# The additive band mask of a windowed attention, entered into PSUM by eight 64x32 tiles instead of two full-array products

## What is computed

```python
def local_attention(q, k, v):           # WINDOW = 32
    ...
    mask = (it < jb) | (it > jb + w) | (jb == -1)
    sim = jnp.einsum('bhwie,bhwje->bhwij', bq, bk2) * QK_SCALE
    sim = jnp.where(mask, -jnp.finfo(sim.dtype).max, sim)
    attn = jax.nn.softmax(sim, -1)
    out = jnp.einsum('bhwij,bhwje->bhwie', attn, bv2)
for i in range(DEPTH):                  # 6
    x = attn_layer(shift_tokens(x), Wqkv[i], q_scale[i], k_scale[i], Wo[i]) + x
    x = ffn_layer(shift_tokens(x), ln_g[i], ln_b[i], W1[i], b1[i], W2[i], b2[i]) + x
```

## Time and profile before

| | |
|---|---|
| median of 3 runs (lowest, highest) | 1658.93 us (1653.15, 1659.83) |
| the profiled execution, its own time | 1655.81 us |
| its span, first to last instruction | 1654.0 us |
| mean granted TensorE clock | 0.979 of full |
| busy share: PE, ACT, POOL, DVE | 90%, 79%, 77%, 74% |
| PE matmuls (and as many weight loads) | 28624 |
| chain that ended last: PE, ACT, DVE, POOL, issue | 51%, 32%, 5%, 5%, 5% |

### The profile page before, as it was taken

The page is one execution under the profiler, slowest core; times in us unless marked ns, Lnnn a source line. Parts: engine busy times, 40 slices in busy tenths (PEclk is TensorE's granted clock), DMA queues, the critical chain, the costliest instruction groups (busy, mean ns, idle before and its releaser), DMA issues.

```text
span 1654.0 us, 68231 instructions
## 1 busy us (share of the span) xinstructions
PE 1485.1 (90%) x28624; PEld 1207.0 (73%) x28624; DVE 1223.0 (74%) x2376; ACT 1314.5 (79%) x4789; POOL 1279.5 (77%) x1540
## 2 busy tenths in 40 slices
PE   6588999999899899999888999999999899999985
PEld 4467777787677688777777777777777777777874
DVE  6676886887687877768876777878688677777762
ACT  3387887987888888878878888888788797887883
POOL 4388787887787888877978878778779787887761
PEclk9699999999999999999999999999999999999998
DMA  4011220112121121212111212112122012111111
GB/s 128 10 48 52 60 56 27 48 49 58 53 62 28 49 58 46 67 35 55 41 42 47 70 41 56 47 30 66 45 66 56 22 41 60 39 41 47 29 47 33
DMA packets 51021, 80.70 MB, mean 49 GB/s; under 512 B 8962, under 2 KB 16948, under 8 KB 50716
## 3 DMA queue, kind: packets, MB, share of 16 engines
q1 hardware_dynamic: 50716, 76.34, 16.6%
HBM read 18.69 MB, written 1.05 MB: 12 GB/s over the span
## 4 chain that ended last, share of the span: by engine, by line
PE 51%; ACT 32%; DVE 5%; POOL 5%; issue 5%; DMA 0%; SPq 0%; DVEq 0%; POOLq 0%
ACT pr L659 13%; PE ps L424 8%; ACT sq L625 5%; PE ps L401 5%; PE ps L408 5%; PE ps L452 4%; PE ps L462 4%; PE ps L434 4%; PE ps L493 4%; PE ps L402 4%; PE ps L403 4%; ACT pT L665 3%; ACT kT L650 3%; PE ps L418 3%; ACT qT L650 3%
## 5 line engine op out<-in xcount | busy, mean ns | idle before, releaser
L799 POOL TENSOR_TENSOR t<-t 128x512 f32<-128x512 f32 x384 | 498.8, 1299 | 203.9 <-DVE t L984 203.8
L659 ACT ACTIVATE pr<-ps,nmax 128x64 f32<-128x64 f32 x1536 | 475.4, 362 | 1.2 <-DVE nmax L999 1.2
L820 POOL TENSOR_TENSOR t<-t,rn 128x512 f32<-128x512 f32 x384 | 392.7, 1044 | 7.5
L659 ACT ACTIVATION_READ_ACCUMULATOR pr<-ps,nmax 128x1 f32 x1536 | 381.1, 257 | 0.0
L982 DVE TENSOR_TENSOR t<-ps,rope 128x512 f32<-128x512 f32 x384 | 263.0, 685 | 144.9 <-PE ps L408 75.0
L625 ACT ACTIVATE sq<-ps 128x512 f32<-128x512 f32 x384 | 240.4, 646 | 60.6 <-PE ps L403 60.0
L401 PE MATMUL ps<-w_hi,xt_hi 128*128 128x512 f32 x576 | 270.7, 470 | 17.0 <-DVE t L984 5.5
L961 DVE TENSOR_REDUCE sums<-sq 128x8 f32<-128x512 f32 x384 | 249.7, 666 | 19.9 <-ACT sq L625 19.9
L984 DVE TENSOR_TENSOR t<-ps,rope 128x512 f32<-128x512 f32 x384 | 261.3, 680 | 0.0
L402 PE MATMUL ps<-w_lo,xt_hi 128*128 128x512 f32 x576 | 230.5, 400 | 1.4 <-issue 1.4
L403 PE MATMUL ps<-w_hi,xt_lo 128*128 128x512 f32 x576 | 231.1, 401 | 0.3 <-issue 0.3
(11 more groups left out here) (123 smaller groups left out, 2764.4 us busy)
## 6 DMA issues: line engine op xcount, KB each, us to landing
v_win<-v SPq DMA_DIRECT2D x384, 128.0 KB, 2.3
wqkv<-wqkv_in SPq DMA_DIRECT2D x36, 256.0 KB, 3.9
xsh<-xr SPq DMA_DIRECT2D x24, 224.0 KB
wo<-wo_in SPq DMA_DIRECT2D x6, 512.0 KB, 3.4
w<-w_in SPq DMA_DIRECT2D x6, 342.0 KB, 4.4
w<-w_in SPq DMA_DIRECT2D x6, 172.5 KB
x<-x_in SPq DMA_DIRECT2D x4, 256.0 KB, 5.9
out<-x SPq DMA_DIRECT2D x4, 256.0 KB, 2.7
```

The costliest lines, as they stand in the source:

```text
L659: i = A(pr[:, c, odd * SPAN:(odd + 1) * SPAN], ps[:, S_BANK[odd], c * SPAN:(c + 1) * SPAN], ACT.Exp, bias=nmax[:, odd, c:c + 1], accum_out ...
L799: G.tensor_tensor(t1[:, c, :], t1[:, c, :], t2[:, c, :], ALU.add).then_inc(qk_added[c], 1)
L820: G.tensor_tensor(w, w, rn[:, par(u), h2, a, :].unsqueeze(2).broadcast_to([P, 8, E]), ALU.mult).then_inc(done, 1)
```

## The change

The mask is entered in the same eight parts of the array as the scores. The part with rows 0 to 63 must give queries 64 to 127 their mask too (groups 2 and 3), and the part with rows 64 to 127 must give it to queries 0 to 63. So the constants get a second copy of the mask with its halves swapped (`np.roll(band, P // 2, 0)`), and `band16` holds both. Per unit there are eight matmuls of 512 columns, each with 64 rows and 32 columns of the array, instead of two on the whole array. The constants' transfer grows from 96 to 128 KB, DVE makes two casts instead of one, and POOL's wait for all constants ahead of its steps goes.

```diff
-    return (0.5 * rope).astype(np.float32), np.concatenate([band, ident], 1)
+    return (0.5 * rope).astype(np.float32), np.concatenate([band, ident, np.roll(band, P // 2, 0)], 1)
-    consts = sb("consts", [P, SPAN + P])
+    consts = sb("consts", [P, SPAN + P + SPAN])
-    band16 = sb("band16", [P, BLOCKS, SPAN], BF16)
+    band16 = sb("band16", [P, 2, BLOCKS, SPAN], BF16)
...
-                for odd in range(2):
-                    mm(ps[:, S_BANK[odd], :], ident16[:], band16[:].rearrange("p c w -> p (c w)"), start=True, stop=False,
-                       skip_group_check=True)
+                for g in range(P // WIN):
+                    for odd in range(2):
+                        r, q = slice(E * odd, E * odd + E), slice(WIN * g, WIN * g + WIN)
+                        rows = slice(E * odd + WIN * (g % 2), E * odd + WIN * (g % 2) + WIN)
+                        mm(ps[q, S_BANK[odd], :], ident16[r, rows], band16[r, int(g // 2 != odd)].rearrange("p c w -> p (c w)"),
+                           start=True, stop=False, skip_group_check=True)
...
-            pool.wait_ge(const_ready, 9)
...
-            V.tensor_copy(band16[:], consts[:, 0:SPAN].unsqueeze(1).broadcast_to([P, BLOCKS, SPAN])).then_inc(const_ready, 1)
+            for k, c in enumerate((0, SPAN + P)):
+                V.tensor_copy(band16[:, k], consts[:, c:c + SPAN].unsqueeze(1).broadcast_to([P, BLOCKS, SPAN])).then_inc(const_ready, 1)
```

More of the change, by code:

```diff
@@ L285, in shift_tokens @@
                 else:
-                    sp.wait_ge(const_ready, 9)
+                    sp.wait_ge(const_ready, 10)
                 for t, n in SHIFT_PARTS:
@@ L574, in _ @@
             pe.wait_ge(ld_const, 64)
-            pe.wait_ge(const_ready, 9)
+            pe.wait_ge(const_ready, 10)
             cross_transpose(0)
@@ L721, in _ @@
             A(ident16[:], ident, ACT.Copy).then_inc(const_ready, 1)
-            act.wait_ge(const_ready, 9)
+            act.wait_ge(const_ready, 10)
             cross_copy_inputs(0)
@@ L1087, in _ @@
             dve.wait_ge(ld_const, 64)
-            V.tensor_copy(band16[:], consts[:, 0:SPAN].unsqueeze(1).broadcast_to([P, BLOCKS, SPAN])).then_inc(const_ready, 1)
+            for k, c in enumerate((0, SPAN + P)):
+                V.tensor_copy(band16[:, k], consts[:, c:c + SPAN].unsqueeze(1).broadcast_to([P, BLOCKS, SPAN])).then_inc(const_ready, 1)
             cross_normalise_x(0)
-            dve.wait_ge(const_ready, 9)
+            dve.wait_ge(const_ready, 10)
             cross_stats_x(1)
```

## The result

The kernel after took 1667.0 us (median of 8 runs, 1663.96 to 1679.2), the kernel before 1659.63 (8 runs, 1653.15 to 1666.58). The ratio is 1.0053, with a 95% interval of 1.003 to 1.0076: slower by half a per cent, 7 us, just over what counts here as no change. The forecast was 1655 with 1642 to 1668.

A forecast was written before the change was run, and what follows sets the result against it. ACT's loop was taken to pace light steps, PE those with feed-forward work. A 13.2 us gain in 56 clean units less 9.1 of losses gave 1651.7 for the profiled execution, 1655 against the median, range 1642 to 1668.

The forecast's parts named there:

- What the mask costs and will cost: First mask to first score on PE: 0.52 us falls to 0.24; gain 0.28 where PE waited, 0.19 elsewhere.
- the passage: PE's switch from the whole array to its parts, 0.09 us; the change moves it ahead of the mask, not away.
- rival 3: The masks issue slowly, 0.06 us each: gain near 0.03 us per clean unit, 1666 us; chance 0.04.
- rival 4: The mask parts don't overlap: gain 0.07 us in fours, or 1770 us in series; chance 0.04 together with rival 3.
- A broken unit gains nought: Where scores break off awaiting an instruction packet, the faster mask only makes PE reach that packet earlier; gain nought.
- rival 1: The gain isn't absorbed: breaks stay at 26 or fewer, or broken units gain too; 1636 us, half way 1646; chance 0.3.
- POOL has room: POOL has 0.55 us spare in the light step, 0.58 in the next, so the mask's gain isn't cut.
- 4 more breaks x 1.75: Twelve more instructions a unit raise the breaks in PE's scores from 26 to 30, a loss of 7.0 us.
- rival 2: More packets hurt than are saved, as 12 instructions make a denser burst: 1666 us, or 1672; chance 0.15.
- Start: DVE's second cast before the first normalisation costs 0.34 us; the larger constants' transfer costs nothing.

The follow-up runs named there:

- Relieving POOL: One of POOL's four small norm refinement operations (adding `threes`) left out: kernel after so 1.0038, kernel before so 1.001, both against the kernel before.
- the masks ahead of the wait: Masks issued before PE's wait for the copies of q and k: kernel before so 0.9957, kernel after so 1.0006, aligned as well 0.9682, against the kernel before.
- the count alone: Kernel before with its masks cut into eight whole-array matmuls of 128 columns, 12 more instructions a unit: 1.0075 against the kernel before.
- the shape with the old count: Kernel after with 3 of 64 score products a unit left out, so as many PE instructions as the kernel before: 0.9985 against it.
- the control: Kernel after with filler in the steps, but 21 instead of 93 matmuls at the start, putting boundaries 204 and 216 behind the mask: 0.9964 against the kernel before.
- the aligned kernels: Filler matmuls ahead of the masks keep packet boundaries out of the stretch behind them: kernel before so 0.976, kernel after so 0.9587, against the kernel before.

## Why the prediction was wrong

Forecast were 4 us less; measured were 7 us more, at the upper end of the range and in the wrong direction. Step by step:

- **What the mask costs and will cost: right.** 0.24 us forecast, 0.21 measured; the passage moved and cost its 0.09. A light step gained 0.33 (forecast 0.28), a long one 0.25 (0.19). The eight masks start within 0.023 us of each other in the records, so rival 3 falls; they are done in 0.41 us, so rival 4 falls too. By the 25 ns between matmuls that the Trainium skill, "TensorE: Matmul & The Clock Gate", section "Wait — 56ns, not 53.3ns?", gives as the floor, eight masks would by estimate need 0.175 us to start; the trace does not agree.
- **A broken unit gains nought: right.** 3.29 and 3.28 us from mask to resumption in the 20th unit; over the 26 broken units the median is 3.4 us before and 3.5 after, so the distance did not shrink with the mask, and rival 1 falls.
- **POOL has room: wrong, and the largest error of the sum.** The step that failed reads "POOL has 0.55 us to spare in the light step and 0.58 in the next, more than the mask can give back, so I don't cut the gain for it". POOL's timeline over these two steps, the kernel before and then the kernel after, first and last row:
```profile
607.75 1.05 POOL L831 TENSOR_TENSOR pr<-pr,rsum 128x512 f32<-128x512 f32 x1
...
634.11 1.28 POOL L799 TENSOR_TENSOR t<-t 128x512 f32<-128x512 f32 x1 [0.26 <-DVE t L984]
```
```profile
869.16 1.04 POOL L835 TENSOR_TENSOR pr<-pr,rsum 128x512 f32<-128x512 f32 x1
...
895.52 1.28 POOL L803 TENSOR_TENSOR t<-t 128x512 f32<-128x512 f32 x1 [0.26 <-DVE t L987]
```
26.36 us in both, and the 0.26 at the end is POOL's only wait in either. What I read as room is mostly some 0.08 us between one small operation and the next, which nobody can use. Two steps therefore took 13.45 + 14.15 = 27.60 us before and 13.12 + 14.57 = 27.69 after: the gain of the light step was handed back in the next. The chain of the kernel after shows the handing back:
```profile
882.48 1.23 POOL t L803
883.71 1.01 POOL pr L835
884.72 0.04 issue
884.77 0.66 PE ps L438 x4
885.42 0.63 PE ps L472 x4
```
PE has its scores done 0.3 us earlier and waits for the probabilities. With this, undisturbed steps in all units give 12.3 us, where I had 23.3. That is 11.0 of the 12.3 us between the forecast (-4.1) and what the two profiled executions show (+8.15). Relieving POOL brought the step back, and the masks ahead of the wait, which saved more in the light steps, lengthened the middle one more. It did not bring the total back, so the 11.0 us is the term's error and not what a faster POOL is worth here.
- **"4 more breaks x 1.75": right in size by luck, wrong in kind.** In the table's terms I had forecast 10.1 us of gain not kept and 8.8 us of further loss, 18.9 in all; 19.6 was measured. But the breaks in the scores did not become 30. They stayed 26 and grew (42.7 to 54.3 us), stops of the instruction stream in all went from 40 to 45, the new ones behind the scores. The clock was not in the sum at all. Steps in which it fell have 22.8 us more excess (17.8 to 40.6), most of it the stops' own time; PE's busy time in them above that of their kind is 9.8 us before and 16.2 after (without the first step), so the clock itself cost some 6 us more. That rival 2's mechanism alone makes the kernel slower was shown by the count alone (1.0075).
- **Start:** 0.34 forecast for the cast and found; the other 0.96 is mostly a transfer that varies between runs.

Beyond the mis-sized terms, the runs showed that terms of such a sum don't add. Three times the undisturbed steps were made 12 to 13 us shorter (the shape, the shape with the old count, POOL relieved), and three times the excess of the profiled execution grew by about as much or more (19.6, 12.6, 20.0). Only when the boundaries were moved out of the bursts did a gain reach the total: 26 us, of which 15.5 can be put down to the shape.

Open: how far ahead a packet is asked for, and so why the units with a boundary at 204 in the control don't break; and which order of DVE's and POOL's work tips the middle step into its longer form. That the longer stop causes the lower clock rests on their standing together in the records; no run changed one without the other, and some stops as long left it at full speed.

## What to carry to other kernels

Before costing a change that adds or removes TensorE instructions, count them between the last semaphore wait and the end of a dense burst, and find where the packets' boundaries fall; moving them out of the burst with cheap filler gave 2.4% here, and 4.1% together with the change, which by itself lost 0.5%. An engine's idle share is no room: follow its timeline over two or three steps, and if it never waits for anyone, it sets the pace of those steps together, whatever the share says. Time saved ahead of something that arrives at its own moment turns into idle time, and here longer stops of PE went, more often than short ones, with a lower granted clock behind them.

## What the hardware showed that I had not expected

- In the 20th and the 48th unit stops of 1.53 and 1.60 us left the clock at 1.00; stops of 1.74 and 2.23 us in the same units were followed by a mean of 0.93 and 1.44 and 1.29 us more of PE busy time (19.90 to 21.34, 19.87 to 21.16).
- Eight matmuls of 512 bf16 columns on eight parts of the array, 64 by 32, are done together in 0.41 us, where one on the whole array took 0.38, though all write into the same two banks.
- In the aligned kernels a boundary 54 to 165 instructions behind the first mask gave no stop in the scores, or one of up to 1.7 us; one at 216 gave a stop of 1.8 to 2.5 us in 22 of 22 units.
